# Gate biases folded into the gate weights, and both layer norms finished by per-row-scalar passes on GpSimd

## The reference

```
e = leaky_relu((x * a_0) @ x.T)          # per graph
p = softmax(where(adj == 1, e, NEG_INF))
y = layernorm(x + p @ x)                 # (v - mean) / sqrt(var + 1e-5)
h = y @ W.T
g = h @ Wg.T
vals = (h + b) * sigmoid(g + bg)
out = layernorm(y + relu(adj.T @ vals))
```

## Time and profile before

| | us |
|---|---|
| median of three runs | 132.91 |
| lowest, highest | 131.42, 133.43 |
| profiled execution, span | 130.9 |
| busy PE, PEld, DVE, ACT, POOL | 113.8, 93.0, 97.7, 99.1, 83.2 |

### The profile page before, as it was taken

One profiled execution on the slowest core, in us unless ns is written; L12 is line 12 of the kernel. 1 busy time (PEld: TensorE's weight loads), 2 busy tenths in 40 slices (PEclk: granted clock), 3 DMA queues, 4 the chain that ended last, 5 costly groups with the idle time before them and its releaser, 6 DMA issues.

```text
span 130.9 us, 3162 instructions
## 1 busy us (share of the span) xinstructions
PE 113.8 (87%) x706; PEld 93.0 (71%) x713; DVE 97.7 (75%) x528; ACT 99.1 (76%) x308; POOL 83.2 (64%) x124
## 2 busy tenths in 40 slices
PE   6838679999999999999999999999999997799300
PEld 6738668669797979797979797979797976575200
DVE  0564489458898989888989898989898988966520
ACT  4447999396979798979797979797979785647522
POOL 4000035527679797978797979797979788491440
PEclk9995999999999999999999999999999999999975
DMA  2999500690082476546656564647474202020222
GB/s 57 306 292 290 138 0 3 191 285 12 0 254 67 117 211 175 148 131 190 176 144 175 145 177 144 200 123 203 118 202 118 80 0 80 8 83 0 80 80 83
DMA packets 34769, 17.29 MB, mean 132 GB/s; under 512 B 1219, under 2 KB 34758, under 8 KB 34758
## 3 DMA queue, kind: packets, MB, share of 16 engines
q1 hardware_dynamic: 34608, 17.17, 46.9%
q10 hardware_dynamic: 150, 0.00, 0.1%
HBM read 12.98 MB, written 4.19 MB: 131 GB/s over the span
## 4 chain that ended last, share of the span: by engine, by line
PE 77%; ACT 9%; DMA 4%; issue 3%; SPq 2%; DVE 2%; ACTq 0%; POOL 0%; POOLq 0%; DVEq 0%
PE p_hg L874 26%; PE p_ag L885 11%; PE p_e L826 10%; PE p_o L851 10%; PE p_hg L871 8%; PE p_yt L860 5%; PE p_ut L841 5%; DMA adj_s<-adj 4%; ACT prob L659 2%; ACT prob_t L669 2%; ACT absent L636 1%; PE p_e L822 1%; ACT xat L648 1%; ACT out_s L688 1%; ACT rel L652 1%
## 5 line engine op out<-in xcount | busy, mean ns | idle before, releaser
L874 PE MATMUL p_hg<-w_both,y_t 128*128 128x256 f32 x128 | 36.2, 405 | 0.0
L874 PEld LDWEIGHTS p_hg<-w_both,y_t 128*128 128x128 f32 x128 | 21.7, 189 | 8.9 <-issue 7.3
L659 ACT ACTIVATE prob<-nscore,nmax 128x128 f32<-128x128 f32 x64 | 24.7, 389 | 0.4 <-DVE nmax L738 0.4
L597 POOL TENSOR_SCALAR rs<-mv 128x4 f32<-128x4 f32 x16 | 3.6, 224 | 32.5 <-DVE mv L766 32.5
L754 DVE SCALAR_TENSOR_TENSOR res<-p_o,rz,x_s 128x128 f32<-128x128 f32 x64 | 18.0, 344 | 7.7 <-issue 4.7
L851 PE MATMUL p_o<-x_s,prob_t 128*128 128x128 f32 x128 | 17.5, 280 | 2.3 <-ACT prob_t L669 2.3
L885 PE MATMUL p_ag<-vals,mask 128*128 128x128 f32 x128 | 17.8, 277 | 1.4 <-issue 1.3
L826 PE MATMUL p_e<-xt,xat 128*128 128x128 f32 x128 | 17.7, 284 | 0.7 <-ACT absent L636 0.4
L826 PEld LDWEIGHTS p_e<-xt,xat 128*128 128x128 f32 x128 | 17.6, 201 | 0.6
L851 PEld LDWEIGHTS p_o<-x_s,prob_t 128*128 128x128 f32 x128 | 15.5, 192 | 3.2 <-ACT prob_t L669 3.2
L599 POOL TENSOR_TENSOR rs<-rs,minus_half 128x4 f32<-128x4 f32 x16 | 16.6, 1041 | 1.5 <-POOL rs L597 0.3
(11 more groups left out here) (65 smaller groups left out, 195.3 us busy)
## 6 DMA issues: line engine op xcount, KB each, us to landing
xt<-x_t SPq DMA_DIRECT2D x16, 256.0 KB, 3.1
adj_s<-adj SPq DMA_DIRECT2D x16, 256.0 KB, 3.5
x_s<-x SPq DMA_DIRECT2D x16, 256.0 KB, 3.9
out<-out_s SPq DMA_DIRECT2D x15, 256.0 KB, 2.3
out<-out_s SPq DMA_DIRECT2D x2, 128.0 KB, 1.8
w_rows<-w SPq DMA_DIRECT2D x1, 192.0 KB, 4.6
wg_s<-wg_t SPq DMA_DIRECT2D x1, 192.0 KB, 4.8
a_col<-a ACTq DMA_DIRECT2D x1, 0.5 KB, 2.9
```

What stands on the lines that cost most here:

```text
L659: nc.scalar.activation(prob[:, k, i], nscore[:, k, i], ACT.Exp, scale=-1.0, bias=nmax[:, s, i:i + 1], accum_out=psumz[:, s, i:i + 1]).then ...
L874: last = nc.tensor.matmul(p_hg[:, i], y_t[:, k, i], w_both[:], start=False, stop=(i % 2 == 1), skip_group_check=True)
```

## The change

Three things are done together.

Biases. On PE, the head adds a fp32 matmul of one row (`mean_row`, all 1/128) with the bias row (256 columns) into the accumulator that becomes `w_both`, so that every row of the gate weights carries 1/128 of the bias. ACT's copy of `y_t` adds 1.0 to each element. Since y now has a mean of zero in each row, and the columns of the centred weights sum to zero, the product holds exactly the bias. The two bias matmuls of each group, `ones3`, `b_parts` and DVE's splitting are gone; each gate matmul starts its own accumulator.

Norms. norm1 and norm2 now have one form: eps, minus the mean, the power, all on [128, 4], and then four passes over [128, 128], one for each graph, which add minus the mean and multiply by the scale in one instruction, both taken from a column of the row's own scalars. PE's turn_y waits for each of the four apart. There is no `cent`, and residual2 of group g waits for the whole norm2 of g-2 where it waited for its first pass.

Tail. The last four groups are treated as the others: ACT's finish is gone, and POOL makes their `out_s`.

```diff
...
@@ -45,8 +44,8 @@
         """, """
         weigh:4 exp:3 absent:4 turned_probs:3 tanh_b:1 tanh_a:1 mask:2 relu:4 turned_y:2
         """, """
-        exp:15 turned_probs:15 tanh_a:13 mask:14 tanh_b:13 turned_y:14 finish:12 tanh_a:14 mask:15 tanh_b:14
-        turned_y:15 finish:13 tanh_a:15 tanh_b:15 finish:14 finish:15
+        exp:15 turned_probs:15 tanh_a:13 mask:14 tanh_b:13 turned_y:14 tanh_a:14 mask:15 tanh_b:14
+        turned_y:15 tanh_a:15 tanh_b:15
         """),
     "vector": (3, """
         scores:0 inverse:0 scores:1 residual1:0 stats1:0 means1:0 inverse:1 scores:2 residual1:1 stats1:1
...
@@ -579,52 +565,42 @@
         def _(pool):
             nc.gpsimd.memset(ident[:], 0.0).then_inc(const_done, 1)
             nc.gpsimd.memset(penalties[:], 0.0).then_inc(const_done, 1)
...
+            nc.gpsimd.memset(mean_row[:], 1.0 / P).then_inc(const_done, 1)
             nc.gpsimd.memset(ones_col[:], 1.0).then_inc(const_done, 1)
...
-            nc.gpsimd.memset(minus_half[:], -0.5).then_inc(cent_done, 1)
+            nc.gpsimd.memset(minus_half[:], -0.5).then_inc(const_done, 1)
             pool.wait_ge(const_done, 2)
             for m, fill in ((ident, 1.0), (penalties, -PENALTY)):
                 nc.gpsimd.affine_select(out=m[:], in_=m[:], compare_op=ALU.not_equal, fill=fill, base=0,
                                         pattern=[[-1, P]], channel_multiplier=1).then_inc(ident_done, 1)
             pool.wait_ge(const_done, 5)
-            pool.wait_ge(cent_done, 1)
             def norm1(g, s):
                 k = s % 2
                 wait_alone(nc.gpsimd, mv1_done, G * (g + 1))
-                nc.gpsimd.tensor_scalar(rs1[:, k, 0], mv1[:, s, :, 1], EPS, None, ALU.add).then_inc(pool1, 1)
-                pool.wait_ge(pool1, 2 * g + 1)
-                nc.gpsimd.tensor_tensor(rs1[:, k, 1], rs1[:, k, 0], minus_half[:], ALU.pow).then_inc(pool1, 1)
-                pool.wait_ge(pool1, 2 * g + 2)
-                nc.gpsimd.tensor_tensor(y[:, s], res1[:, k], rs1[:, k, 1, :, None].broadcast_to([P, G, P]),
-                                        ALU.mult).then_inc(y_done, 1)
+                nc.gpsimd.tensor_scalar(rs1[:, k, 0], mv1[:, s, :, 1], EPS, None, ALU.add).then_inc(var1_done, 1)
+                nc.gpsimd.tensor_scalar(minus1[:, k], mv1[:, s, :, 0], -1.0, None, ALU.mult).then_inc(minus1_done, 1)
+                pool.wait_ge(var1_done, g + 1)
+                nc.gpsimd.tensor_tensor(rs1[:, k, 1], rs1[:, k, 0], minus_half[:], ALU.pow).then_inc(rstd1_done, 1)
+                pool.wait_ge(minus1_done, g + 1)
+                wait_alone(nc.gpsimd, rstd1_done, g + 1)
+                for i in range(G):
+                    nc.gpsimd.tensor_scalar(y[:, s, i], res1[:, k, i], minus1[:, k, i:i + 1], rs1[:, k, 1, i:i + 1],
+                                            ALU.add, ALU.mult).then_inc(y_done, 1)
             def norm2(g, s):
                 k = s % 2
                 wait_alone(nc.gpsimd, mv2_done, G * (g + 1))
-                nc.gpsimd.tensor_scalar(rs2[:, s, 0], mv2[:, s, :, 1], EPS, None, ALU.add).then_inc(pool2, 1)
-                if is_late(g):
-                    nc.gpsimd.tensor_tensor(shift[:, s, 0], mv2[:, s, :, 0], minus_one[:], ALU.mult).then_inc(shift_done, 1)
-                    pool.wait_ge(pool2, 2 * g + 1)
-                    nc.gpsimd.tensor_tensor(rs2[:, s, 1], rs2[:, s, 0], minus_half[:], ALU.pow).then_inc(pool2, 1)
-                    pool.wait_ge(pool2, 2 * g + 2)
-                    pool.wait_ge(shift_done, 2 * (g - n_groups + LATE) + 1)
-                    nc.gpsimd.tensor_tensor(shift[:, s, 1], shift[:, s, 0], rs2[:, s, 1], ALU.mult).then_inc(shift_done, 1)
-                    return
-                if not is_first(g):
-                    pool.wait_ge(out_done, g)
-                nc.gpsimd.tensor_tensor(cent[:], res2[:, k], mv2[:, s, :, 0:1].broadcast_to([P, G, P]),
-                                        ALU.subtract).then_inc(cent_done, 1)
-                pool.wait_ge(pool2, 2 * g + 1)
-                nc.gpsimd.tensor_tensor(rs2[:, s, 1], rs2[:, s, 0], minus_half[:], ALU.pow).then_inc(pool2, 1)
-                pool.wait_ge(pool2, 2 * g + 2)
-                pool.wait_ge(cent_done, g + 2)
+                nc.gpsimd.tensor_scalar(rs2[:, k, 0], mv2[:, s, :, 1], EPS, None, ALU.add).then_inc(var2_done, 1)
+                nc.gpsimd.tensor_scalar(minus2[:, k], mv2[:, s, :, 0], -1.0, None, ALU.mult).then_inc(minus2_done, 1)
+                pool.wait_ge(var2_done, g + 1)
+                nc.gpsimd.tensor_tensor(rs2[:, k, 1], rs2[:, k, 0], minus_half[:], ALU.pow).then_inc(rstd2_done, 1)
+                pool.wait_ge(minus2_done, g + 1)
                 if not is_first(g, 2):
                     pool.wait_ge(stored[k], 16 * ((g - k) // 2))
-                nc.gpsimd.tensor_tensor(out_s[:, k], cent[:], rs2[:, s, 1, :, None].broadcast_to([P, G, P]),
-                                        ALU.mult).then_inc(out_done, 1)
+                wait_alone(nc.gpsimd, rstd2_done, g + 1)
+                for i in range(G):
+                    nc.gpsimd.tensor_scalar(out_s[:, k, i], res2[:, k, i], minus2[:, k, i:i + 1], rs2[:, k, 1, i:i + 1],
+                                            ALU.add, ALU.mult).then_inc(out_done, 1)
             run("gpsimd", {"norm1": norm1, "norm2": norm2})
             general_pool(pool)
...
@@ -662,7 +638,7 @@
             def evac_ut(g, s):
                 if is_first(g):
-                    act.wait_ge(w_pe, 2)
+                    act.wait_ge(w_pe, 1)
                     nc.scalar.activation(w_both[:, 0:P], p_hg[:, 0, 0], ACT.Copy, scale=0.5).then_inc(w_ready, 1)
                     nc.scalar.activation(w_both[:, P:2 * P], p_hg[:, 0, 1], ACT.Copy).then_inc(w_ready, 1)
                 act.wait_ge(tu_done, g + 1)
...
@@ -670,48 +646,25 @@
             def evac_yt(g, s):
                 act.wait_ge(ty_done, g + 1)
-                nc.scalar.activation(y_t[:, s % 2], p_yt[:], ACT.Copy).then_inc(yt_done, 1)
+                nc.scalar.activation(y_t[:, s % 2], p_yt[:], ACT.Copy, bias=1.0).then_inc(yt_done, 1)
             def tanh(g, s, h):
                 act.wait_ge(hg_done[h], g + 1)
                 nc.scalar.activation(th[:, s % 2, half(h)], p_hg[:, half(h), 1], ACT.Tanh, scale=0.5)\
                     .then_inc(tanh_done[h], 1)
-            def finish(g, s):
...
-                k = s % 2
-                act.wait_ge(shift_done, 2 * (g - n_groups + LATE) + 2)
-                act.wait_ge(pool2, 2 * g + 2)
-                act.wait_ge(r2_done, g + 1)
...
-                for i in range(G):
-                    nc.scalar.activation(out_s[:, k, i], res2[:, k, i], ACT.Identity, scale=rs2[:, s, 1, i:i + 1],
-                                         bias=shift[:, s, 1, i:i + 1]).then_inc(finish_done, 1)
...
             nc.scalar.dma_start(a_col[:], a_0).then_inc(a_loaded, 16)
-            nc.scalar.dma_start(b_rows[:], b_loop.broadcast_to([3, 2 * P])).then_inc(b_loaded, 16)
...
-            act.wait_ge(cent_done, 1)
+            nc.scalar.dma_start(b_rows[:], b_loop).then_inc(b_loaded, 16)
+
+            act.wait_ge(const_done, 5)
             nc.scalar.activation(table_loader[:], minus_half[:, 0:1], ACT.Exp).then_inc(table_loaded, 1)
             run("scalar", {"weigh": weigh, "turned_probs": evac_ut, "absent": absents, "mask": masks, "relu": rel,
-                           "turned_y": evac_yt, "exp": exps, "tanh_a": of_half(tanh, 0), "tanh_b": of_half(tanh, 1), "finish": finish})
+                           "turned_y": evac_yt, "exp": exps, "tanh_a": of_half(tanh, 0), "tanh_b": of_half(tanh, 1)})
             general_scalar(act)
         @block.vector
         def _(dve):
             nc.vector.memset(warm[:], 0.0).then_inc(warm_ready, 1)
...
-            dve.wait_ge(b_loaded, 16)
...
             dve.wait_ge(w_loaded, 16 * 2)
             nc.vector.bn_stats(w_stats[:], w_rows[:, LOOP]).then_inc(w_step, 1)
...
@@ -776,10 +716,8 @@
                 k = s % 2
                 dve.wait_ge(ag_done[0], g + 1)
                 dve.wait_ge(ag_done[1], g + 1)
-                if not is_first(g, 2) and not is_late(g - 2):
-                    dve.wait_ge(cent_done, g)
-                if is_late(g) and is_late(g - 2):
-                    dve.wait_ge(finish_done, G * (g - 1 - n_groups + LATE))
+                if not is_first(g, 2):
+                    dve.wait_ge(out_done, G * (g - 1))
                 nc.vector.scalar_tensor_tensor(out=res2[:, k], in0=p_ag[:], scalar=0.0, in1=y[:, s],
                                                op0=ALU.max, op1=ALU.add).then_inc(r2_done, 1)
...
@@ -833,9 +771,14 @@
                 k = s % 2
                 if is_first(g):
                     pe.wait_ge(w_step, 3)
-                    nc.tensor.transpose(p_hg[:, 0, 0], w_mid[:], ident[:]).then_inc(w_pe, 1)
-                    nc.tensor.matmul(p_hg[:, 0, 1], w_mid[:], wg_s[:, LOOP], start=True, stop=True)\
-                        .then_inc(w_pe, 1)
```

(17 more changed lines are left out.)

72 lines of the change are left out of this document (17 added, 55 removed).

## The result

The changed kernel takes 145.19 us (median of 4 runs, 143.61 to 145.64) where the kernel before takes 132.62 beside it: 1.098 of the time before, with an interval of 1.089 to 1.106. The forecast was 126.8 and faster. The execution profiled has a span of 143.8 us, 12.9 more than before.

The account below looks back on a forecast made before the run. PE was taken to bound the kernel at 6.53 us a period, DVE next at 6.11. From the 130.9 us span, 4.2 (body), 0.6 (head) and 1.3 (tail) leave 124.8; plus 2.0 gives 126.8 us, range over cases 125.0 to 141.2.

Parts of the forecast that it names:

- 1.52 + 4x: POOL's time for one norm: small instructions, power and semaphore 1.52 us, plus four passes of x; 2.92 us forecast.
- x: Start-to-start time of one [128, 128] POOL pass with two operations and two per-row scalars; taken as 0.35 us, range 0.28 to 0.52.
- The middle: Body of the program: period 6.15 us, 0.38 less than before, over 11 periods, 4.2 us gained.
- the points at which they were to decide (0.41, 0.47): Values of x on POOL: forecast holds up to 0.41, rival 1 from 0.41 to 0.47, rival 2 from 0.47 on.
- rival 2: POOL makes the kernel slower: x of 0.52, +8.3 us, 141.2 us; chance 0.25.
- rival 1: POOL becomes the bound and eats the gain: x from 0.41 to 0.47, 132.3 us at 0.44; chance 0.18.
- ends 0.64 and 1.0: Low and high estimates of what PE saves a period without bias matmuls; 0.9 us was taken.
- Its own rings: Two wait loops, residual1 over norm1, ACT and PE, and norm2 over store and load; each 6.1 us a period at x = 0.35.
- residual2's longer wait: DVE's residual2 waits for the whole norm2 two groups earlier; claimed to cost nothing, with cover of most of a period.
- +0.9: Head, PE: added fp32 bias-row matmul and turning of weights at the 1.2 GHz level, 0.9 us longer.
- 0.6 gained: Head in sum: longer weights' preparation against two groups' shorter gates and DVE's waits, 0.6 us gained.
- Forecast -1.3: Tail: group 15's gates 0.9 us shorter and norm2:15 0.4 us shorter, 1.3 us gained.

## Why the prediction was wrong

**The step that failed** is the sum for one norm on POOL, 1.52 + 4x with x = 0.35. Both of its terms were too small. x is 0.433, which costs 4 x 0.083 = 0.33 us a norm. The fixed part is 1.90: eps to minus is 0.32, not 0.2; the first pass starts 1.25 to 1.34 after the power and not 1.14; the last pass and the next norm's start stand 0.10 further apart than starts of passes do. That is 0.38 on the mean. (As the prediction lists them, its own terms add up to 1.54.) The norm is 3.635 and not 2.92; with the early waits for DVE it is 3.655, and 27 of them are 19.8 us more than forecast. 5.3 of these went into the idle time that the forecast left POOL (84.1 us for 27 norms of 2.92, 78.8), and 14.5 into the time. The middle was forecast at -4.2 and came out at +10.4: a difference of 14.6. (The stretches measured do not begin and end exactly where the terms of the forecast do; by norm1:15's own lengthening they differ by up to 0.5.)

**x.** It was read off a row without per-row scalars (the select, 0.28), a row of two-input passes (0.43), and their middle. The second input of those passes is a [128, 4] tile spread over the columns, so no row showed two full inputs either. The runs give the parts: 0.155 fixed, 0.107 for 128 columns, 0.09 and 0.08 for the two scalars. The Trainium skill's rule that small read commands cost some 102 cycles each (GPSIMD Engine Reference, Performance pitfalls for Q7 kernels) had spoken against this edit. At that page's 1.2 GHz this is an estimate of 0.085 us, and the 0.09 and 0.08 measured agree with it in size; that the scalars are fetched by such commands is not shown. The prediction added the two reads to 0.35 and got 0.52, since no row showed the pass without them; it is 0.263, and with them 0.433. I gave that case a quarter and went with the middle of two rows, neither of which had the operand that was in question.

**The fixed part** was taken from one row, the eps ahead of a large pass at 65.40, and used for every pair of small instructions. I treated it as known, put no range on it, and set all rivals by x alone. So the points at which they were to decide (0.41, 0.47) were wrong: with the true fixed part the old period is reached at 4x = 3.27 - 1.90, x = 0.34, below my own forecast for it. At the forecast x of 0.35 the same sum gives a period of 6.60, so no gain at all against 6.53. The direction of rival 2 came true (POOL is the bound, no idle time between norm2 and norm1, slower by more than its 8.3 us), by its mechanism but at an x that I had counted as rival 1.

**PE and DVE** came out near the forecast. The gates are 0.86 shorter (2.82 to 1.96; forecast 0.9, ends 0.64 and 1.0). Without biases the kernel before takes 127.38, near the 126.8 that the forecast gave to the whole change. That the two numbers are close is in part luck: the period is 6.22 and not 6.15, and beside DVE it is a ring over ACT and PE that holds it there, which the prediction did not list by itself. Its own rings, over a norm and over the store and the reload, and residual2's longer wait play no part that shows: in the body POOL leaves no gap between norms.

**Head.** The prediction counted +0.9 on PE less two shorter gates and DVE's waits, and so 0.6 gained. Instead norm1:2 starts 1.8 later in this pair of profiles, 2.5 over all. The preparation took 1.5 longer on PE (2.17 for 0.64), and norm1:1 started 2.65 later (24.87 for 22.22). The gates did give their part back: norm1:2 starts 5.41 after norm1:1 where it was 6.25, 0.84 less, and it is 5.41 too in the kernel before without biases and 5.89 in the changed kernel with the bias matmuls back. So the term that failed is the +0.9. It priced the added matmuls alone and took the low clock to end where it did before. It stayed at the 1.2 GHz level longer, where attend:0 took 0.91 more and the next scores 0.86 more (1.91 for 1.05). That the added matmuls keep it there is what the mean clocks above suggest, 0.68 or 0.79 with them and 0.79 to 1.00 without; with one profile of each kernel and an overlap at 0.79 it is likely and not proven.

**Tail.** Forecast -1.3, measured +0.7. The last gates were to be 0.9 shorter and took 3.63, where biases and gates took 2.81 (118.34 to 121.15): the granted clock is 0.5, the 1.2 GHz level, in the slice from 129.4 us, after PE waited 2.24 us for POOL's y. norm2:15 takes 3.62 (137.85 to 141.47) and not 2.92.

**What stays open.** Why a small TENSOR_SCALAR behind another costs 0.32 where it costs 0.19 ahead of a two-input instruction, and why the replacement of the second also lets the next norm start 0.11 sooner: the runs show the sizes, not the reason. The pass behind the power waits 0.2 to 0.3 in every form of the changed kernel tried, two-input passes included. In the kernel before y's pass waits less than 0.1, and the last pass of norm2 less than 0.1 in most turns and 0.2 to 0.3 in the others. That was not taken apart.

## What to carry to other kernels

Before work is moved to another engine, write that engine's whole stage out instruction by instruction and put a range on the gaps between small instructions too; here they cost as much as the misjudged passes did. Look for rings that pass through several engines as well, since relieving one engine may lead straight into one. A pass on POOL with per-row scalars is priced by columns, by a fixed part and by each scalar, so four passes of 128 columns are not one of 512. A bias folded into weights is not free where it needs a mean of zero that nobody took out before: ask which engine pays, and whether the engine that is relieved had a second one right behind it.

## What the runs showed of the hardware

- POOL, TENSOR_SCALAR with add and multiply on [128, 128] fp32: 0.263 us start to start with immediates, 0.355 with one scalar from a tile, 0.433 with two; 0.84 ns a column beyond the fixed part. A two-input pass whose second input is a [128, 4] tile spread over 512 columns takes 1.65 ns a column.
- The same with subtract and multiply and two scalars from a tile: 0.78 us.
- POOL, [128, 4]: TENSOR_SCALAR to TENSOR_SCALAR 0.32 us, TENSOR_SCALAR to TENSOR_TENSOR 0.19 to 0.20, TENSOR_TENSOR to TENSOR_TENSOR 0.15.
- PE, in the chain of waits: the bf16 bias matmul of 3 rows and 512 columns takes 0.32 us behind fp32 ones, and two side by side take 0.53; the one of 128 rows takes 0.22 behind fp32 ones. The gates (eight records) take 1.92 in one stretch and 2.12 in two with a bf16 matmul ahead of each.
- PE's granted clock between 8 and 24 us: 0.68 or 0.79 in the nine kernels whose head folds the bias in, 0.79 to 1.00 in the five others.
